# Reciprocal roots of the norms in the token blocks: a power operation on GpSimd in place of a seed and three refinement steps

## What is computed

```
x = _layernorm(x + _L0_attn_ref(x, ...))   # Mamba block: inner RMS norm over 256, own layer norm
x = _layernorm(x + _L0_ffn_ref(x, ...))    # attention with switched experts
x = _layernorm(x + _L1_attn_ref(x, ...))   # linear attention with rope, own layer norm
x = _layernorm(x + _L1_ffn_ref(x, ...))    # soft mixture of experts
def _layernorm(x, axis=-1, eps=1e-05):
    m = mean(x); v = var(x)
    return (x - m) / sqrt(v + eps)
# inside the Mamba block
y = y * rsqrt(mean(y * y, axis=-1) + EPS) * norm_w
...
return (y - mu) * rsqrt(var + EPS) * ln_w + ln_b
```

## Time and profile before

| | us |
|---|---|
| median of 3 runs | 1499.7 |
| lowest and highest | 1496.85 and 1500.32 |
| span of the profiled execution (first to last instruction) | 1497.5 |
| PE busy | 1440.1 |
| DVE busy | 1218.1 |
| POOL busy | 751.1 |

### The profile page before, as it was taken

The page is one execution under the profiler, slowest core; times in us unless marked ns, Lnnn a source line. Parts: engine busy times, 40 slices in busy tenths (PEclk is TensorE's granted clock), DMA queues, the critical chain, the costliest instruction groups (busy, mean ns, idle before and its releaser), DMA issues. The chain is left out here.

```text
span 1497.5 us, 32591 instructions
## 1 busy us (share of the span) xinstructions
PE 1440.1 (96%) x10940; PEld 1269.0 (85%) x10940; DVE 1218.1 (81%) x2359; ACT 821.0 (55%) x1850; POOL 751.1 (50%) x1833
## 2 busy tenths in 40 slices
PE   8889999999999999999999999987999999998998
PEld 6658888888888888888888887867999999998997
DVE  5778889889898898898898887768888888857664
ACT  4354454555454455455554544315777767677775
POOL 1433346355354454453463452226777777457772
PEclk8789999999999999999999999998999999999999
DMA  5100000000000000000000003006777777887872
GB/s 193 60 8 8 1 15 2 15 16 1 15 5 12 15 5 12 15 1 15 16 1 15 9 1 127 1 1 166 188 187 192 196 192 192 263 335 296 310 304 75
DMA packets 135426, 130.43 MB, mean 87 GB/s; under 512 B 7232, under 2 KB 125248, under 8 KB 128768
## 3 DMA queue, kind: packets, MB, share of 16 engines
q1 hardware_dynamic: 135296, 128.79, 27.8%
HBM read 72.93 MB, written 55.84 MB: 86 GB/s over the span
## 5 line engine op out<-in xcount | busy, mean ns | idle before, releaser
L737 PE MATMUL ps_l<-ve_f,oe 128*128 128x128 f32 x2048 | 275.7, 279 | 0.8 <-DVE ve_f L1741 0.8
L737 PEld LDWEIGHTS ps_l<-ve_f,oe 128*128 128x128 f32 x2048 | 248.8, 192 | 23.1 <-issue 20.5
L1741 DVE SCALAR_TENSOR_TENSOR ve_f<-ps_s,oT 128x512 f32<-128x512 f32 x248 | 166.4, 679 | 4.1 <-PE ps_l L737 2.3
L2935 POOL TENSOR_TENSOR d_s<-d_ex 128x1024 f32<-128x1024 f32 x31 | 125.3, 4041 | 83.2 <-ACT d_ex L2685 83.2
L1702 DVE COPY_PREDICATED vals<-oh,ps_l 128x1024 f32<-128x1024 int32 x112 | 146.8, 1311 | 17.2 <-PE ps_l L477 15.1
L2560 PE MATMUL ps_s<-d_ex,arena 128*128 128x128 f32 x1024 | 121.5, 278 | 7.0 <-DVE d_ex L2828 7.0
L2560 PEld LDWEIGHTS ps_s<-d_ex,arena 128*128 128x128 f32 x1024 | 118.7, 194 | 7.4 <-DVE d_ex L2828 7.4
L475 PE MATMUL ps_l<-veH,x1H 128*128 128x512 f32 x256 | 115.4, 451 | 0.8 <-DVE vals L1702 0.7
L1293 ACT ACTIVATE ve_f<-ps_l,r 128x128 f32<-128x128 f32 x128 | 47.3, 369 | 125.7 <-DVE r L1714 125.4
L2548 PE MATMUL ps_l<-arena 128*128 (+1 forms) x960 | 112.2, 275 | 2.3 <-ACT d_raw L2680 2.3
L2548 PEld LDWEIGHTS ps_l<-arena 128*128 128x128 f32 x960 | 109.6, 192 | 2.5 <-ACT d_raw L2680 2.5
(11 more groups left out here) (332 smaller groups left out, 3865.8 us busy)
## 6 DMA issues: line engine op xcount, KB each, us to landing
logits<-d_raw SPq DMA_DIRECT2D x128, 256.0 KB, 3.5
e_lt<-logits SPq DMA_DIRECT2D x32, 1024.0 KB, 5.2
y_slots<-d_ys SPq DMA_DIRECT2D x64, 256.0 KB, 4.6
d_ex<-y_slots SPq DMA_DIRECT2D x8, 1024.0 KB, 6.9
e_y<-y_slots SPq DMA_DIRECT2D x6, 1024.0 KB, 6.8
d_w<-W SPq DMA_DIRECT2D x16, 256.0 KB, 3.4
arena<-xT SPq DMA_DIRECT2D x16, 128.0 KB, 2.4
arena<-x SPq DMA_DIRECT2D x16, 128.0 KB, 2.5
```

The lines of the kernel that those rows point to most:

```text
L737: last = pe.matmul(ps_u[:, cols], oe[:, hp, e, :], mo[:, n % MO, hp, :], start=False, stop=(e == NE - 1 and hp == HP - 1), skip_group_chec ...
L1741: V.scalar_tensor_tensor(mo[:, n % MO, :, :].rearrange("p a n -> p (a n)"), chosen_of(b, c), float(NE - e), oT[:, u, c, :, :].rearrange("p ...
L2935: G.tensor_tensor(s8[:], part[:, 0:8, :], part[:, 8:16, :], ALU.add).then_inc(n, 1)
```

## The change

In `token_blocks`, `rsqrt` calls a new helper `root` wherever it called `newton` without `fused`. `root` has two instructions: variance plus eps into `v` (as before, but with the scale 1.0), then `v` to the power of a tile `half` that holds -0.5, into `y`. The second raises the semaphore by 13, so all waits on it keep their numbers. The scale 1/256 that rms had in the first instruction goes into ACT's squares (0.5 / sqrt(256) in place of 0.5; the sum is the mean then). `half`, 128x2 numbers, is filled once at POOL's start. DVE's three roots of the last block and all of `soft_experts` stay as they are.

```diff
+def root(pool, wait_apart, done, k, source, var, eps, half, v, y):
+    wait_apart(pool, source)
+    pool.tensor_scalar(v[:], var, 1.0, eps, ALU.mult, ALU.add).then_inc(done, 1)
+    wait_apart(pool, (done, k + 1))
+    pool.tensor_tensor(y[:], v[:], half[:], ALU.pow).then_inc(done, RSQRT_OPS - 1)
...
+        half = sb("half", [C])
...
         def rsqrt(pool, n, b, scale, eps, source, per, fused=False):
             _, _, v, y, t = nbuf[n]
-            newton(pool, wait_both, norms[n]["rstd"], RSQRT_OPS * b, (source, per * b + per), var_of(n), scale, eps,
-                   v, y, t, fused)
+            if fused:
+                newton(pool, wait_both, norms[n]["rstd"], RSQRT_OPS * b, (source, per * b + per), var_of(n), scale, eps,
+                       v, y, t, fused)
+            else:
+                root(pool, wait_both, norms[n]["rstd"], RSQRT_OPS * b, (source, per * b + per), var_of(n), eps,
+                     half, v, y)
...
-                    nc.scalar.activation(sq[:], yg[:, c, :], ACT.Square, scale=0.5, accum_out=ssq[:, c:c + 1]
+                    nc.scalar.activation(sq[:], yg[:, c, :], ACT.Square, scale=0.5 / math.sqrt(DI), accum_out=ssq[:, c:c + 1]
...
         @block.gpsimd
         def _(pool):
             G = nc.gpsimd
+            G.memset(half[:], -0.5)
```

## The result

The changed kernel takes 1510.25 us (median of 4 runs, 1506.33 to 1512.92); the kernel before, run on the same chip beside it, takes 1498.73 us (4 runs, 1496.85 to 1500.32). The ratio is 1.0075, with a 95% interval of 1.0056 to 1.0093: slower by 11.5 us. The profiled execution spans 1511.2 us and is the longest of the four.

What follows compares the result with a forecast made beforehand. TensorE was taken to bound the kernel from 150 to 850 us, leaving mainly the ramp. Gains of 2.85 + 0.5 + 0.6 + 0 = 3.95 us turned the 1499.7 us median into 1495.8 us, range 1492.4 to 1500.3 us.

Steps and rivals of the forecast that it cites:

- What bounds the kernel: 150 to 850 us: PE is busy 696.84 of 700 us, so TensorE sets the pace whatever the other engines do.
- What is removed: All 93 roots: 12 of 14 instructions go, some 235 us of POOL's time, nearly all covered by PE's own work.
- below nothing it cannot be: Each root's added power: bounded by 0.21 and 4.04 us; it stands in the seed's place, so cannot cost less than nothing.
- The added operation: One power on a 128x2 tile per root, taken as 1.0 us, with 0.2 and 4.0 us kept as range.
- The slow power: Powers from 4.25 us on make POOL late in every block: 1545 us at 5 us, near 1590 at 6; chance 0.13.
- the middling one: Each power costs 2 to 4 us, so gains in blocks 0, 1 and 14 shrink: 1497 to 1499.7 us; chance 0.11.
- the one-time price: Block 0's rms: the first power pays one delay, free up to 4.5 us; 1497.3 or 1497.8 us; chance 0.05.
- Block 0, ln2: In the ramp, `a_ln2` starts at about 55.1 us instead of 57.95: 2.85 us gained, 3.14 us at most.
- Block 1: Its ln1: DVE's wait goes and its scalings no longer meet `b_vg`; 0.5 us gained, ends 0 and 1.9 us.
- Block 14: Its lnB: DVE comes 0.62 us earlier to its scalings at 919.06 us, and PE gains 0.6 us.
- The clock: Ramp, from 59 us: granted clock of 0.50 follows PE's idle time; counted as 0, up to 2.0 us possible.
- the rival: Clock stays up from 59 to 72 us: 2.0 us more, 1493.8 us, or 1492.4 with block 1's 1.9; chance 0.24.

Runs made afterwards that it cites:

- e1: The changed kernel with POOL's `b_vg` held in the slots until DVE has made `kv`; 1493.45 us, ratio 0.9963 to the kernel before.
- e3: The changed kernel with rms's roots made by Newton steps as before, the other 77 by powers; 1495.27 us, ratio 0.9977 to the kernel before.
- e5: The changed kernel with `b_vg` held only until DVE has made `qr`; 1501.30 us, ratio 1.0019 to the kernel before.
- e6: The changed kernel with `b_vg` as an operation of one tensor input, the gate's factor left out; 1496.55 us, ratio 0.9987 to the kernel before.
- e7: The changed kernel with `qr` reading its first operand from PSUM, the product with the sines left out; 1500.19 us, ratio 1.0007 to the kernel before.
- e10: The changed kernel without a hold, `b_vg` moved behind ln1's root in POOL's list; 1503.14 us, ratio 1.0022 to the kernel before.
- e8_seed_only: The kernel before, without powers, with rms's root in the slots cut to its seed; 1507.82 us, ratio 1.0058 to the kernel before.
- e2: The kernel before, without powers, with one Newton step instead of three in rms's root in the slots; 1511.98 us, ratio 1.0105 to the kernel before.

## Why the prediction was wrong

It forecast 1495.8 us in a range of 1492.4 to 1500.3 us; the time is 1510.25 us.

**What bounds the kernel: right, but read too far.** TensorE does set the pace from 150 to 850 us. The step that failed is the sentence under "What is removed": nearly all of it "is worth nothing by itself, because PE's own work covers it". It looked only at who waits for the roots, and asked of each root what an earlier end would bring its reader. It did not ask what POOL does next. POOL runs its list in order. The rms root took 5.2 us in the block shown (417.38 to 422.62 us) and now takes 1.35 us (418.64 to 419.99 us), so `b_vg` starts 0.37 us ahead of `qr` instead of 3.44 us behind it. DVE loses 1.31 us by that, and each block 1.04 us. (The prediction had 4.1 us for a root, though the rms root in the earlier trace rows takes 5.25 us, so it also took the shift for smaller than it is.) In "below nothing it cannot be" only the duration of the power was bounded; the effect of the earlier neighbour was given no bound and no rival.

**The signs were in the rows.** The prediction used this very mechanism twice: for the 1.05 us row of POOL beside `veL` in block 0, and for block 1, where it explained DVE's 2.04 us by `b_vg` beside it and counted its going away as a gain. Both times it asked what a meeting that is there costs, and not which new one an earlier start makes. The Trainium skill (Advanced Engine Details and Errata, VectorE Performance Modes), cited there, was applied to the new instruction and not to the one that the change moves. A row of rms's own Newton chain, 0.69 us instead of 0.20 beside `qr`, says the same for the block at 419 us; the Newton chain itself had stood on top of `qr` and the convolution steps before, in pieces of 0.2 us with pauses, and had cost DVE nothing that shows. With the rows at hand a rival could have been priced: `qr` and a pair of convolution steps beside `b_vg`, whose two instructions last 2.04 us together. The sign that it named itself also answered: PE's busy time from 150 to 850 us was to stay within a microsecond of 697 us, and it is 683.45 us.

**The added operation: right.** The power was taken as 1.0 us; it measured 0.69 us, and 0.78 us in rms (0.69 us stays where nothing runs beside it). The 1.0 us was a guess between 0.2 and 4.0 us, and no run shows by what steps the chip makes a power. POOL's busy time fell by 200.7 us (751.1 to 550.4); the some 150 us of the prediction would by its own working be 161. The slow power and the middling one fall. So does the one-time price: the very first power, at 37.86 us, took 0.72 us. The estimate of about 6 us by the Trainium skill (GPSIMD Engine Reference, Instruction dispatch) has no counterpart in this trace.

**Block 0, ln2: right.** Expected 55.1 us with the power delayed by 0.85 us beside `veL`; measured 54.97 us, with a power of 1.48 us (0.69 + 0.79) and no idle time ahead. The power ended at 54.93 us, within 0.1 us of DVE's own queue, so the whole wait of 3.14 us is gone; the 2.98 us are less because this trace was 0.18 us later already. The turning of x1 was expected at 56.4 us:

```profile
56.26 0.44 PE L612 MATMUL ps_s<-id_f,x 128*128 128x128 f32 x2
```

**Block 1: nearly nothing instead of 0.5 us, and not by the mechanism.** The prediction had `b_vg` past when DVE comes. But `b_vg` waits for DVE's own `vals`, the row just ahead of the scaling, and so it still starts beside it:

```profile
89.79 2.05 POOL L2240 TENSOR_TENSOR vals<-vals,gx 128x512 f32<-128x512 f32 x2 [2.52 <-DVE vals L1716]
```

The wait of 0.44 us went, and the pair takes 1.32 us instead of 2.04 (89.60 us). The next row of DVE pays in its place, with 1.17 us for 0.42:

```profile
90.95 1.17 DVE L1666 TENSOR_TENSOR na<-na,lnw 128x256 f32<-128x256 f32 x1
```

The lead at 98.79 us is the 2.9 us that block 0 had already given. The lower end of that term was the true one.

**Block 14: as said, and lost in the rest.** The 0.62 us of waiting are gone from the row at 928.12 us.

**The clock: the forecast's case here, the rival's in part elsewhere.** Granted clock and busy times, changed kernel, 59 to 61 us:

```profile
59.00:60.00 1.00, 0.19 (x1) 0.22 (x2) 1.00 (x4) 0.00 (x0) 0.00 (x0) 0.71 0.00 0
60.00:61.00 1.00, 1.00 (x5) 1.00 (x6) 1.00 (x2) 0.00 (x0) 0.00 (x0) 0.50 0.00 0
```

It falls to 0.50, the lower level of 1.2 GHz, all the same, 0.6 us later than before. The idle time of 3.26 us ahead of the turning of x1 is gone, but PE idled 0.76 and 1.46 us before 60 us. It stays there for 6.8 us (59.4 to 66.2) instead of 10.2 us (58.8 to 69.0), and yet DVE's wait for PE is still 2.06 us (2.01 in the earlier trace rows), and block 1's `a_ln2` comes 43.8 us behind block 0's, as before. So in this execution the rival gets nothing. The other traces show that this is not so in every execution: with a power in ln2 the low stretch is 6.8 us in three (this one, e1, e3) and 3.4 us in four (e5, e6, e7, e10). In those four DVE waits 0.60 to 0.71 us, and the way from one `a_ln2` to the next is 42.4 to 42.7 us. In all five traces with Newton's root in ln2 the low stretch is 10.2 us and the way 43.5 to 44.0 us. Some 1.1 to 1.4 of the rival's 2.0 us thus come back in some executions.

**The sum as a whole.** What it added up for the ramp, 3.95 us, is what the runs give once the collision is out of the way: e1_hold_kv is 0.37% (5.5 us by the ratio, 3.6 to 7.5 by its interval) faster, e3_rms_newton 0.23% (3.4 us, 0.9 to 5.8). The prediction priced the instructions it shortened and left out the one behind them. That its sum agrees is in part luck: block 1's 0.5 us did not come, and block 0 gave a little more than said.

**The version that beats both.** It is e1_hold_kv, 1493.45 us: the change as it is, and `b_vg` held until DVE has written `kv`.

## What to carry to other kernels

When a chain on one engine is shortened, write down the next instruction in that engine's list, its new start, and what DVE does at that time; cover by the bounding engine protects against a late POOL, not against a POOL that works at the wrong moment (here it forgave 0.23 to 0.28 us a block of what DVE lost). If the next instruction is a large one on GpSimd, place it (by a wait on a result that is due anyway) beside DVE steps that read PSUM or are small, and look at the durations of unchanged instructions first when the profile of a shorter kernel is longer. Moving it elsewhere in the list only helps if no DVE step of the kinds named below stands there.

## What the runs showed of the hardware

- **A DVE instruction with two SBUF operands and a POOL instruction run by turns rather than side by side.** `qr` (128x512) 0.69 us alone, 1.21 us in the changed kernel, up to 1.54 us in e8_seed_only; the pair of 128x256 convolution steps 0.87 and 1.66 us (1.73 in e7_qr_psum); the 128x256 sum of lnC 0.42 and 1.13 us. POOL pays as well: `b_vg` 2.04 and 2.49 us.
- **Each waits for the end of the other's running instruction.** `qr` ends 0.54 us behind the POOL instruction that was running when it came, whatever was left of that: behind 421.00 us in the changed kernel, 415.11 us in e6_one_input, 421.54 us in e8_seed_only. A delayed convolution step ends 0.27 to 0.29 us behind POOL's (changed, e2, e5, e6, e7, e8), and the second instruction of `b_vg` 0.90 to 0.91 us behind `qr` (changed, e8). The most that one DVE instruction lost is 0.86 us, under the 1.04 us of one of POOL's.
- **One operand in PSUM frees a two-operand instruction of it:** `qr` at 0.69 us wholly beside `b_vg` (e7_qr_psum), the 128x512 step at 0.68 us between two delayed ones (e5_hold_qr). The Trainium skill (GPSIMD Engine Reference, Specifications) names DVE instructions with two SBUF inputs, beside those in a two-port mode, as the ones that contend with GpSimd; these rows agree for two SBUF inputs, and give the size.
- **A scaling with one SBUF tensor operand meets POOL too:** a pair of 128x128 takes 0.60 us alone (101.71 us), 1.22 us beside POOL's `a_am` of 57.86 us in block 0 and 2.04 us beside `b_vg`. The statistics of 128x128, also with one operand, keep their 0.49 us beside `b_vg` (e1_hold_kv).
- **Tiny POOL instructions suffer as well.** The power on 128x2 took 1.48 us beside `veL` against 0.69 us, and a Newton step of 0.20 us took 0.69 us.
- **A power of 128x2 elements on GpSimd** costs 0.69 us, that is a bit more than three plain two-input operations of this size at 0.21 us.
